# GpSimd rests by clearing a buffer, in place of waiting for the experts' progress

## The reference

```
x = x + 0.5 * ffn(layernorm(x));  x = x + attn(layernorm(x));  x = x + 0.5 * ffn(layernorm(x))

ffn(x):  t = rmsnorm(x) * scale;  g = t @ gate_w.T + gate_b
         vals, idx = top_k(g, 4);  w = softmax(vals)              # 4 of 32 experts per token
         h1 = t @ w1[e].T + b1[e]                                 # 128 -> 256, halves interleaved
         h  = swiglu(h1);  y_e = h @ w2[e].T + b2[e]              # 128 -> 128
         return x + sum over the 4 experts of w_e * y_e
attn(x): q, k = softmax over the features of two stacked projections;  v = x @ Wv.T + bv
         16 heads of 8 features, scores divided by their row sum (linear attention), 256 tokens each
```

## Time and profile before

| | us |
|---|---|
| median of 3 runs | 881.05 |
| lowest and highest | 872.26, 893.66 |
| the profiled execution | 867.46 |
| its span, first to last instruction | 865.7 |
| TensorE busy in it | 550.6 |
| GpSimd busy in it | 514.6 |
| VectorE busy in it | 439.8 |
| ScalarE busy in it | 351.6 |

### The profile page before, as it was taken

The page is one execution under the profiler, slowest core; times in us unless marked ns, Lnnn a source line. Parts: engine busy times, 40 slices in busy tenths (PEclk is TensorE's granted clock), DMA queues, the critical chain, the costliest instruction groups (busy, mean ns, idle before and its releaser), DMA issues.

```text
span 865.7 us, 12809 instructions
## 1 busy us (share of the span) xinstructions
PE 550.6 (64%) x3182; PEld 452.3 (52%) x3183; DVE 439.8 (51%) x1246; ACT 351.6 (41%) x752; POOL 514.6 (59%) x537
## 2 busy tenths in 40 slices
PE   6055948898988787475406761889798988760000
PEld 4042347787877676254303551678687877660000
DVE  7837133444455657357782766335454555631045
ACT  5233314454554554565405651445455545420000
POOL 3467676666246566657566667566623666667771
PEclk9555988999999998777557955899998999866555
DMA  7991114454545453111111112445444555313221
GB/s 274 425 375 42 44 64 135 151 176 152 164 148 162 152 163 116 55 42 50 41 40 45 47 45 73 127 153 173 152 158 137 166 164 155 111 58 102 53 55 52
DMA packets 54179, 108.13 MB, mean 125 GB/s; under 512 B 12576, under 2 KB 19968, under 8 KB 53248
## 3 DMA queue, kind: packets, MB, share of 16 engines
q1 hardware_dynamic: 37760, 74.13, 25.6%
q0 software_dynamic: 16384, 33.59, 13.2%
HBM read 51.00 MB, written 56.62 MB: 124 GB/s over the span
## 4 chain that ended last, share of the span: by engine, by line
PE 32%; issue 18%; another core or an unknown queue 17%; DVE 14%; ACT 9%; POOL 7%; DMA 1%; ACTq 1%; DVEq 0%; POOLq 0%
PE PS L1190 10%; PE PS L1180 8%; PE PS L1081 6%; POOL YG L517 6%; DVE X L933 4%; ACT hidT L589 3%; DVE glulin L882 2%; PE PS L1281 2%; PE PS L1098 1%; ACT swish L624 1%; PE PS L1207 1%; ACT xT L593 1%; PE PS L1240 1%; DVE topi L726 1%
## 5 line engine op out<-in xcount | busy, mean ns | idle before, releaser
L517 POOL DMA_INDIRECT YG<-ys,row x256 | 251.1, 981 | 181.4 <-issue 78.0
L494 POOL DMA_INDIRECT xs<-U,row x256 | 256.4, 1002 | 151.8 <-issue 68.6
L1180 PE MATMUL PS<-W,xT 128*128 x768 | 189.2, 391 | 0.0
L882 DVE TENSOR_SCALAR glulin<-PS 128x512 f32<-128x512 f32 x96 | 66.4, 691 | 198.7 <-PE PS L1190 85.9
L1180 PEld LDWEIGHTS PS<-W,xT 128*128 128x128 f32 x768 | 143.6, 197 | 18.2 <-issue 1.6
L1190 PE MATMUL PS<-W,hidT 128*128 x768 | 111.8, 291 | 63.3 <-ACT hidT L589 56.7
L1190 PEld LDWEIGHTS PS<-W,hidT 128*128 128x128 f32 x768 | 100.3, 199 | 87.0 <-issue 84.9
L581 ACT ACTIVATE yrow<-PS 128x512 f32<-128x512 f32 x96 | 57.3, 597 | 171.4 <-PE PS L1190 75.7
L895 DVE SCALAR_TENSOR_TENSOR hid<-glulin,swish 128x512 f32<-128x512 f32 x96 | 66.6, 694 | 16.5 <-ACT swish L585 10.6
L1081 PE MATMUL PS<-ident,xrow 128*128 128x128 f32 x384 | 61.4, 286 | 15.8 <-DMA xrow<-xs 8.0
L593 ACT ACTIVATE xT<-PS 128x512 f32<-128x512 f32 x96 | 56.6, 590 | 34.3 <-issue 32.3
(11 more groups left out here) (168 smaller groups left out, 645.8 us busy)
## 6 DMA issues: line engine op xcount, KB each, us to landing
xrow<-xs SPq DMA_DIRECT2D x96, 256.0 KB
ys<-yrow SPq DMA_DIRECT2D x96, 256.0 KB
xs<-YG SPq DMA_DIRECT2D x6, 2048.0 KB, 13.7
W<-in_w12T SPq DMA_DIRECT2D x1, 6144.0 KB
xs<-U,row POOLq DMA_INDIRECT x256
YG<-ys,row POOLq DMA_INDIRECT x256
out<-X SPq DMA_DIRECT2D x7, 256.0 KB
X<-in_x SPq DMA_DIRECT2D x4, 256.0 KB, 3.7
```

What stands on the lines that cost most here:

```text
L494: pool.indirect_dma_start(out=xs[c], out_offset=bass.IndirectOffsetOnAxis(ap=row[:, i:i + 1], axis=0), in_=U[:, (c * CT + t) * H:(c * CT + ...
L517: pool.indirect_dma_start(out=YG[:, t * TOPK + k, :], out_offset=None, in_=ys[c], in_offset=bass.IndirectOffsetOnAxis(ap=row[:, i:i + 1], ...
L882: v.tensor_scalar(glu[:, s, :].rearrange("p (q f) -> p q f", q=GT), h1[:, 0], LIMIT, None, ALU.min).then_inc(glu_ready, 1)
L1180: last = te.matmul(h1, xT[:, s, q * P:(q + 1) * P], W[:, bass.ds(es[q], 2 * H)], start=True, stop=True)
```

## The change

The helper `keep_to_experts` is removed. In its place a helper `rest` puts a memset of 128 partitions by 256 fp32 columns, a buffer `spread` that nothing reads, before each of the same 256 DMAs (64 in the scatter of chunk 1 and 64 in the gather of chunk 0, in both mixtures). A new semaphore `rested` is raised by each memset, and each memset waits for the one before it, since they write the same buffer. The DMAs keep all their other waits, and so do the stretches beside the front and beside attention.

```diff
+        spread = sb("spread", [P, 256])
...
+        rested = sem("rested")
...
-            def keep_to_experts(f, c, i):
-
-                k, part = divmod((36 * i + (2750 if c else -50)) // 10, 10)
-                if k < 1:
-                    return
-                if part >= 7 and k < NGF:
-                    pool.wait_ge(xT_ready, f * NGF + k + 1)
-                elif part >= 5 and k >= 3:
-                    pool.wait_ge(hidT_ready, f * NGF + k - 2)
-                elif part >= 2:
-                    pool.wait_ge(turned, f * (NGF + 3) + k + 1)
-                elif k > 1:
-                    pool.wait_ge(multiplied, f * (NGF + 2) + k - 1)
+            rests = [0]
+
+            def rest():
+                wait_count(pool, rested, rests[0])
+                rests[0] += 1
+                g.memset(spread[:], 0.0).then_inc(rested, 1)
...
                         if c:
-                            keep_to_experts(ph // NCHUNK, 0, t * TOPK + k)
+                            rest()
...
                         if c == 0:
-                            keep_to_experts(ph // NCHUNK, 1, t * TOPK + k)
+                            rest()
```

## The result

The changed kernel takes 1034.22 us (median of four runs, 1023.50 to 1046.60) against 880.38 us for the kernel before in the same group (also four runs, the three of the table above among them): a ratio of 1.174, interval 1.157 to 1.192. The forecast was 867 us with a range up to 900. The profiled execution took 1023.5 us, its span is 1021.8 us and TensorE's granted clock in it 0.756.

A forecast was written before the change was run, and what follows sets the result against it. The start of GpSimd's last gather was taken to set the end. It moves 13.8 us earlier, so the profiled 867.46 us becomes 853.7; keeping the median's 13.6 us distance gives 867 us, range 845 to 900.

The forecast's parts named there:

- What bounds: Whole kernel: the last gather's start sets the end, 102.5 us before it; late TensorE signals lose 0.75 us per experts' step.
- Waits removed, clears added: GpSimd's four runs beside experts: 1.25 us without waits, plus 0.26 per clear and 0.02, a pitch of 1.53 us.
- bounds 1.25 and 1.86: GpSimd's pitch in us: 1.25 if the clear hides wholly, 1.86 if it adds its span and a start of its own.
- Effect on signals: Experts' steps: silence before every DMA and no unpaused runs, so half the present loss, 3.9 us per step.
- The bound above: Experts' steps: 7.11 us for a stalled step as upper bound, against 3.49 with no stall.
- the prediction's own signs of being wrong: Pitch under 1.45 or over 1.6, growing VectorE and ACT waits with unknown releaser, or experts' steps staying at 4.2 or more.
- The ports: Clears writing SBUF beside VectorE: cost nothing, covered by its idle time; without that cover 0.7 us per step.
- Rival 1: TensorE's signals to ACT and VectorE are held longer: one step in three stalls, 3.6 us each, 922 us; chance 0.17.
- Rival 3: The clear hides in the 0.30 us before a DMA, GpSimd is no bound, the experts are: 853 us; chance 0.14.
- Rival 2: GpSimd's clear costs more than its spacing: 907 us at pitch 1.70, 947 at 1.86; chance 0.13.
- The sum: Scatters, gathers and experts' stages added up: first load of group 24 at 226.0, last gather at 749.4, 13.8 us earlier.

The follow-up runs named there:

- e6: The changed kernel with clears of 320 columns in place of 256: 941.9 us, ratio 1.062 to the kernel before.
- e3: The changed kernel with clears of 384 columns in place of 256: 877.3 us, ratio 1.003 to the kernel before.
- d2: The changed kernel without its clears, so neither waits nor clears, run once more on a chip of the first kind: 1100.6 us, ratio 1.268 to the kernel before.
- e2: The changed kernel with the waits of before called again behind each clear of 256 columns: 867.8 us, ratio 0.994 to the kernel before.
- e1: The changed kernel without its clears, so neither waits nor clears beside the experts: 1099.3 us, ratio 1.259 to the kernel before.
- c1: The kernel before, unchanged, run again for a trace, on a chip of the second kind: 754.5 us, ratio 1.002.

## Why the prediction was wrong

**What bounds.** Right in the place: it named late signals of TensorE as what sets the experts' steps, and the end as set by the start of the last gather. The accounting above goes by that chain.

**Waits removed, clears added.** The clear costs less than was taken. Its span is 0.33 us, but the DMA behind it starts 0.17 us after its end where it stands 0.30 behind another DMA, so it adds 0.33 + 0.17 - 0.30 = 0.20, not 0.26: pitch 1.47 and 1.45, forecast 1.53, bounds 1.25 and 1.86. A small miss in microseconds with a large effect, as e6 and e3 show; yet e6, whose scatter has the forecast pitch, lost 6% too, so a right pitch would not have saved the forecast. The Trainium skill's advice to take spacing rather than spans (page "Perfetto Trace Analysis", section "GPSIMD Engine Instruction") misled only in the choice of rows: memsets behind memsets are not a memset between DMAs.

**Effect on signals: the step that failed.** "I take half the present loss, 3.9 us per step", by the reading that the clears give silence before each DMA and break up the unpaused ones. The steps were 5.73 and 6.20 over the stage, and 8 to 13 us while GpSimd issued. The waits' silence was not what let signals through; the waits kept the mean pitch at 1.54 to 1.58, and 1.46 is too short on these chips. The reading failed at the earlier trace rows: I took 251.81 as 1.2 us of silence after the last DMA, and d2 has the same release, 7.10 us after the gather's first DMA, with no silence at all. The bound above, one stalled step of 7.11 us, was no bound: nothing in one stall says what happens when the DMAs go on at that distance for 64 of them. Two of the prediction's own signs of being wrong came true with it: the waits with an unknown releaser grew (72.9 to 176.9 us), and the steps stayed over 4.2.

**The ports.** The clears beside VectorE cost nothing, as taken (e2, and VectorE's busy time of 439.4).

**The rivals.** Rival 1 named the place and the sign, with "the deciding quantity may be unpaused runs, not silence" as what spoke against it. Neither was it. Its 922 us are too little because it added a stall of 3.6 us to one step in three. Rival 3 thought GpSimd harmless at a pitch of 1.25; e1 is that case, 1099 us and not 853. Rival 2 asked what a longer clear costs, and had the sign of it reversed on these chips: e3 is 157 us faster than the changed kernel, though its price for GpSimd as the bound was near (877 us at 1.6 to 1.7, forecast 907 at 1.70). On the other chips, where nothing is held, that rival is what happens: 1.07 and 1.10.

**The sum.** The last DMA of scatter one started at 224.46, forecast 222.8 (the run began 5.4 us later than forecast, at a shorter pitch). The load of group 24 came at 267.70, 4.3 us before its copy to xT as in the kernel before, forecast 226.0: the experts were 42 us late for it.

**What stays open.** That too short a mean distance of GpSimd's DMAs holds TensorE's signals is shown on these chips; what is overrun is not. If something is worked off at one DMA per 1.40 us, as e1 and d2 suggest, then beside the experts' steps, where the limit lies near 1.55, TensorE's own signals would have to take part of it; that is a guess. It is not the transfer: over the 64 DMAs of the first scatter beside the experts, the first packet starts on average 1.70 us after its instruction in the changed kernel and 1.74 us in the kernel before, and never later than 2.74. Nor does it hold all signals. This is VectorE's wait for ACT, from the waits of the changed kernel (us in total, times, longest):

```profile
DVE hid L890 <- ACT swish L580: 14.2, 60, 0.5
...
DVE glulin L877 <- remote: 258.8, 33, 13.3
```

These are idle times, which hold the other engine's work too. The records of the semaphores give the delays themselves, for the experts stages of the changed kernel: all 681 of ACT, VectorE and GpSimd come 0.01 us after the instruction's end, while 69 of TensorE's 180 come more than 0.3 us after it, the latest 11.6.

Nothing names what differs between the chips. The traces do differ in one thing beside the late signals: for the same kernel, the trace of before holds 6088 records of semaphore updates and that of c1 14229. In all traces from chips of the first kind there are 6088 to 7622, in the others 14229 to 14557. Most of the missing ones are of DMAs. This may be one more sign of the same overload. It may also be that recording takes part in holding the signals: every run on record has a recorded span and clock, so no run tells what these kernels take unrecorded. That rival stands untested.

Three statements of the Trainium skill bear on this, and none settles it. The page "Perfetto Trace Analysis", section "Tensor Engine Instruction (MATMUL, LD_WEIGHTS)", says that a matmul's signal is pushed only when PSUM has acknowledged the last write, after the modelled end: a place where TensorE's signals could be held and others not; no run here looks into it. Its section "DMA Instruction — SWDGE (GPSIMD)" says that the end of a GpSimd DMA in the profile is the end of the descriptor writing, and what follows is hidden. In d2 the packets after that end took 1.2 of the 9.64 us, so they are not what the signal waits for. The page "SBUF — State Buffer", section "Who interferes with whom", says that a DMA never contends with a compute engine. In the durations the trace agrees (`yrow` takes 597 ns before and 598 after). That section is about ports and says nothing of signals, and it is there that these chips lose the time.

## What to carry to other kernels

When one engine's signals arrive late beside another's DMAs, measure the mean start-to-start distance over a whole run of them, and vary it with everything else kept: here one size of a clear moved the kernel from 1034 to 877 us. Then give the same mean in another shape (bunched, or with less moved), to tell the mean from the single pause. A release that follows the last DMA doesn't show that the pause released it; look for the same signal in a run that doesn't pause. A pause tied to the other side's progress adapts its length to the chip and the stage, a fixed one does not; a fixed one sits on a cliff on the side where it is short. A stall seen once is no upper bound for a stall that may pile up. And where a kernel stands at such a limit, look at it on a second chip before a size is settled.

## What the runs showed of the hardware

- Medians of the kernel before were 872 to 886 us in four groups of runs, on at least three chips, and 752 and 754 in two, on two other chips. The traces show the same durations (an indirect DMA 0.94 to 0.96 us, `yrow` 598 ns), and differ in the late signals and in the number of semaphore updates recorded.
- On the chips of 872 to 886 us, TensorE's signals beside the experts come up to 4.0 us late in the kernel before, 11.6 in the changed one and 57 to 61 us without waits and clears (e1, d2), by the records of the semaphores; those of ACT, VectorE and GpSimd in the same stages 0.01 us after the end.
- A memset of 256, 320 and 384 columns beside DMAs lasts 0.33, 0.38 and 0.44 us. The indirect DMA that follows starts 0.17 us after its end, and 0.30 after another DMA's.
- An indirect DMA of 64 rows keeps GpSimd for 0.90 us, one of 128 rows for 0.96.
